# First expert layer of a four-layer model on one core: dense experts replaced by tiles of chosen token-expert pairs

## The reference, cut to what matters

```python
probs = softmax(xf @ gate_w.T)                    # 16 experts
_, idx = top_k(probs + gate_b, 6)                 # 6 of 16 per row
weights = take_along_axis(probs, idx)
for e in range(16):                               # hidden size 176
    h = silu(xf @ W1[e].T + B1[e]) * (xf @ W3[e].T + B3[e])
    y += cw[:, e:e+1] * (h @ W2[e].T + B2[e])     # cw is 0 where e was not chosen
y += shared(xf)                                   # hidden size 352, every row
```

## Time and profile before

| | us |
|---|---|
| median of 3 runs | 1162.48 |
| lowest, highest | 1162.35, 1163.56 |
| the profiled execution, its own time | 1165.65 |
| its span, first to last instruction | 1163.9 |
| PE busy (share of the span) | 990.9 (85%) |
| DVE busy | 672.4 (58%) |
| ACT busy | 354.6 (30%) |
| POOL busy | 353.8 (30%) |
| mean granted TensorE clock | 0.911 |

### The profile page before, as it was taken

How to read it: one execution, slowest core, us unless ns; L and a number is a source line. 1 busy time by engine, 2 the same in 40 slices (tenths; PEclk the granted TensorE clock), 3 DMA queues, 4 the chain that set the end, 5 groups by cost and what they waited for, 6 DMA issues and landing times. The chain is left out here.

```text
span 1163.9 us, 14272 instructions
## 1 busy us (share of the span) xinstructions
PE 990.9 (85%) x5133; PEld 795.6 (68%) x5133; DVE 672.4 (58%) x1105; ACT 354.6 (30%) x541; POOL 353.8 (30%) x244
## 2 busy tenths in 40 slices
PE   2999999868779999999788995967726869999996
PEld 2677787658568899998667894755615656566664
DVE  4466666545385556655634888968677853222221
ACT  2234443222522333333223442334313432222121
POOL 2577776400122222222100220153235310512222
PEclk9899999969889999999878996969956988999999
DMA  3111120001111111110081001000010019622220
GB/s 113 72 39 39 38 77 0 1 1 35 45 46 46 46 45 45 45 45 18 2 256 61 29 1 33 1 1 1 0 41 1 1 53 399 245 63 42 40 34 10
DMA packets 21473, 61.40 MB, mean 53 GB/s; under 512 B 4401, under 2 KB 12866, under 8 KB 19074
## 3 DMA queue, kind: packets, MB, share of 16 engines
q1 hardware_dynamic: 17346, 56.55, 14.3%
q0 software_dynamic: 4080, 4.22, 2.2%
HBM read 55.50 MB, written 9.21 MB: 56 GB/s over the span
## 5 line engine op out<-in xcount | busy, mean ns | idle before, releaser
L914 DVE SCALAR_TENSOR_TENSOR ffn_HF<-ffn_U,ffn_BIAS,ffn_HG 128x512 f32<-128x512 f32 x54 | 40.4, 750 | 82.5 <-ACT ffn_HG L797 82.4
L87 PE MATMUL ffn_DN<-ffn_WDS_hi,ffn_HS_hi 128*128 128x256 f32 x288 | 83.6, 290 | 3.9 <-DVE ffn_HS_lo L922 3.3
L797 ACT ACTIVATE ffn_HG<-ffn_G,ffn_UB 128x512 f32<-128x512 f32 x54 | 37.1, 690 | 160.5 <-PE ffn_U L89 160.1
L2160 PE MATMUL ffn_GU<-ffn_W,ffn_XTB 128*128 x184 | 85.0, 605 | 0.1
L88 PE MATMUL ffn_DN<-ffn_WDS_lo,ffn_HS_hi 128*128 128x256 f32 x288 | 83.3, 289 | 0.0
L89 PE MATMUL ffn_DN<-ffn_WDS_hi,ffn_HS_lo 128*128 128x256 f32 x288 | 83.2, 289 | 0.0
L767 POOL TENSOR_TENSOR ffn_WDS_lo<-ffn_WD,ffn_WDS_hi 128x1024 fp32r<-128x1024 f32 x9 | 22.1, 2461 | 200.2 <-ACT ffn_WDS_hi L787 200.2
L929 DVE SCALAR_TENSOR_TENSOR X<-ffn_DN,ffn_CG,X 128x256 f32<-128x256 f32 x144 | 67.3, 480 | 20.6 <-PE ffn_DN L89 12.5
L1980 POOL DMA_INDIRECT out_x<-ffn_YB,ffn_XB x23 | 35.9, 1560 | 113.7 <-DVE ffn_YB L2109 111.7
L464 DVE TENSOR_TENSOR attn_RP<-attn_QB,attn_COS 96x1024 f32<-96x1024 f32 x32 | 39.0, 1218 | 51.3 <-PE attn_QB L89 51.2
L2098 DVE COPY ffn_XTB<-ffn_XP 128x256 f32<-128x256 f32 x23 | 9.8, 425 | 88.0 <-PE ffn_XP L2169 88.0
(11 more groups left out here) (432 smaller groups left out, 2759.6 us busy)
## 6 DMA issues: line engine op xcount, KB each, us to landing
ffn_W<-in_f_w SPq DMA_DIRECT2D x9, 1536.0 KB, 27.9
attn_W<-in_L_pairs SPq DMA_DIRECT2D x8, 1088.0 KB, 5.0
ffn_WU<-in_f_up SPq DMA_DIRECT2D x9, 768.0 KB, 4.2
ffn_WD<-in_f_down SPq DMA_DIRECT2D x9, 512.0 KB, 3.5
expert_rows<-in_rows_empty SPq DMA_DIRECT2D x1, 2967.0 KB, 14.4
ffn_XB<-expert_rows SPq DMA_DIRECT2D x23, 129.0 KB, 2.1
ffn_STAGE<-in_f_w SPq DMA_DIRECT2D x1, 2048.0 KB, 8.2
ffn_STAGE<-in_L_pairs SPq DMA_DIRECT2D x2, 768.0 KB, 7.3
```

Source lines behind the costliest of these rows:

```text
L87: pe.matmul(out, a[0], b[0], start=first, stop=False)
L797: act.activation(HG[:, k % 2, :], G[:, k % 2, :], ACT.Silu, bias=bias).then_inc(silu_done, 1)
L914: dve.scalar_tensor_tensor(out=HF[:, k % 2, :], in0=U[:, k % 2, :], scalar=BIAS[:, bass.ds(e * (2 * NC) + 2 * m + 1, 1)], in1=HG[:, k % 2, ...
L2160: last = pe.matmul(GU[:, m, :], x, weights(e, k * 2 * HID3 + m * HID3, HID3), start=k == 0, stop=k == KD - 1)
```

## The change

`experts` is removed, and `routed_many` computes the same part by chosen pairs in plain float32. 8 items do the shared expert (hidden size 352, one tile of rows each). The 6144 pairs are sorted by expert into tiles of 128, at most 63 of them (`TILES0`). No rows are sorted in DRAM: XN is written out as it is, with the row's 16 weights behind it (`rows0`), and a list `IDX` of row numbers, 128 for each tile, is made on chip, by comparisons on DVE (`mark`, 8 of 128x2048 bf16) and 128 small matmuls on PE (`enlist`), while the shared items run. POOL gathers each tile's rows by that list with an indirect DMA, eight tiles ahead into twelve buffers, and scatters each result with addition, even tiles into `sum_a` (the residual with the shared part, written there first) and odd tiles into `sum_b` (zeros); a scatter waits for the one two before it. The last block of the layer ends when POOL has issued the last scatter. `latent_chain` then loads both sums, adds and measures them on DVE at the end of round 0, and takes the norm a round later. The order of a routed item on PE is up, turning the next rows, turning the hidden values of the item before, down for the item two before; on DVE bias, copy of the next rows, product; on ACT silu, copy, and the weighing of the item two before. Three DMAs from DRAM to DRAM (the table of layer 3, the zeros for `sum_b`, a zero row) go to SP's queue in the first attention block. The clearing after the int8 part goes, and one comes behind the first attention. The diff, cut to its core (the indents are cut too):

```diff
+E0, TOP0, HID0 = 16, 6, 176
+TILES0 = B * S * TOP0 // P + E0 - 1
+ROW0 = D + E0
+UP0 = KD * 2 * HID0
...
+    sp.dma_start(DR["rows3"][:, :], A["rows_empty"]).then_inc(scratch_set, 16)
+    sp.dma_start(DR["sum_b"][:, :], A["zeros"]).then_inc(scratch_set, 16)
+    sp.dma_start(DR["rows0"][B * S:B * S + 1, :], A["zero_row"]).then_inc(scratch_set, 16)
     with sp.Fori(1, NP) as p:
         sp.wait_ge(w_lo[2], p)
...
-    def experts(tag, gate, NE, NC, E, TOP, biased):
...
-    NORM_AFTER = 1
+    NORM_AFTER = 2
...
+    if g == 1:
+        for i, (dst, src) in enumerate(((X, "sum_a"), (XN, "sum_b"))):
+            sp.wait_ge(sums_done[i], 16 * ((TILES0 + 1 - i) // 2))
+            sp.dma_start(dst[:, :, :], DR[src].rearrange("(t p) d -> p t d", p=P)).then_inc(taken[i], 16)
...
+    if g == NORM_AFTER - 1:
+        act.wait_ge(measured, T)
+        nrm["deviation"](act)
     if g == NORM_AFTER:
         nrm["scalar"](act)
...
+    if g == 0:
+        for i in range(2):
+            dve.wait_ge(taken[i], 16)
+        for t in range(T):
+            dve.tensor_tensor(X[:, t, :], X[:, t, :], XN[:, t, :], ALU.add).then_inc(whole, 1)
+            dve.wait_ge(whole, t + 1)
+            measure(dve, stats, t).then_inc(measured, 1)
+    if g == NORM_AFTER - 1:
+        nrm["vector"](dve)
...
-    sp.dma_start(rows_dram[:, :], A["rows_empty"]).then_inc(xs_set, 16)
...
+    def routed_many(gate):
+        E, NT, NB, NY, HID, ROW = E0, TILES0, 12, 4, HID0, ROW0
+        ITEMS = T + NT
...
+    MARK_AT = {1: (0, 1), 2: (2, 3), 3: (4,), 4: (5,), 5: (6, 7)}
+    LIST_AT = {3: (0, 1), 4: (2, 3), 5: (4, 5), 6: (6, 7)}
...
+    sp.wait_ge(xn_ready, T)
+    sp.dma_start(DR["rows0"][0:B * S, 0:D].rearrange("(t p) d -> p t d", p=P), XN[:, :, :]).then_inc(rows_out, 16)
+    sp.dma_start(BIAS[:, :], A["f0_bias"]).then_inc(bias_in, 16)
+    for e in range(E):
+        sp.dma_start(W[:, e, :], A["f0_w"][e]).then_inc(w_in, 16)
+    sp.wait_ge(weights_ready, 1)
+    sp.dma_start(DR["rows0"][0:B * S, D:ROW].rearrange("(t p) d -> p t d", p=P), CW[:, :, :]).then_inc(weights_out, 16)
+    sp.wait_ge(shared_added, T)
+    sp.dma_start(DR["sum_a"].rearrange("(t p) d -> p t d", p=P), X[:, :, :]).then_inc(base_out, 16)
...
+    def gather(i):
+        if i >= NB:
+            pool.wait_ge(y_ready, i - NB + 1)
+            pool.wait_ge(x_turned, i - NB + 1)
+        pool.indirect_dma_start(XB[:, i % NB, :], None, DR["rows0"][:, :], bass.IndirectOffsetOnAxis(ap=IDX[:, i:i + 1], axis=0)).then_inc(rows_in[i % NB], 16)
+    def scatter(i):
+        pool.wait_ge(y_ready, i + 1)
+        if i >= 2:
+            pool.wait_ge(sums_done[i % 2], 16 * (i // 2))
+        pool.indirect_dma_start(DR["sum_b" if i % 2 else "sum_a"][:, :], bass.IndirectOffsetOnAxis(ap=IDX[:, i:i + 1], axis=0),
+                                YB[:, i % NY, :], None, bounds_check=B * S - 1, oob_is_err=False, compute_op=ALU.add).then_inc(sums_done[i % 2], 16)
+    pool.wait_ge(rows_out, 16)
+    pool.wait_ge(weights_out, 16)
+    pool.wait_ge(idx_ready, 1)
+    AHEAD = NB - 4
+    for i in range(AHEAD):
+        gather(i)
+    pool.wait_ge(base_out, 16)
+    for i in range(NT):
+        if i + AHEAD < NT:
+            gather(i + AHEAD)
+        scatter(i)
...
+    def weigh(n, e):
+        i = n - T
+        act.wait_ge(down_done, n + 1)
+        if i >= NY:
+            act.wait_ge(sums_done[i % 2], 16 * ((i - NY) // 2 + 1))
+        act.activation(YB[:, i % NY, :], DN[:, n % 2, 0:D], ACT.Copy, scale=XB[:, i % NB, bass.ds(D + e, 1)]).then_inc(y_ready, 1)
+    for n in range(ITEMS + 2):
+        if n < ITEMS:
+            silu(n)
+        if 1 <= n <= ITEMS:
+            h_copy(n - 1)
+        if n - 2 == T:
+            act.wait_ge(owners_out, 1)
+        if n - 2 >= T:
+            weigh(n - 2, act.value_load(EI[0:1, n - 2 - T:n - 1 - T], min_val=0, max_val=E - 1))
...
+    dve.tensor_tensor(OHA[:, t % NM, :, :], PLACESB[:, :, :],
+                      POSB[:, t, :].unsqueeze(1).broadcast_to((P, P, E)), ALU.is_equal).then_inc(places_marked, 1)
...
+    dve.tensor_tensor(GB[:, n % 2, :], GU[:, n % 2, 0:2 * HID], BIAS[:, bass.ds(e * (2 * HID), 2 * HID)], ALU.add).then_inc(biased, 1)
...
+    src = GU[:, 1, 0:2 * HID] if n < T else GB[:, n % 2, HID:2 * HID]
+    dve.tensor_tensor(h_rows(n)[:, 0:hidden(n)], src, HG[:, n % 2, 0:hidden(n)], ALU.mult).then_inc(h_full, 1)
...
+    dve.tensor_copy(XTB[:, n % 2, :], XP[:, 0:D]).then_inc(x_out, 1)
...
+    for n in range(ITEMS):
+        if n == T:
+            dve.wait_ge(bias_in, 16)
+        if n >= T:
+            add_bias(n, dve.value_load(EI[0:1, n - T:n - T + 1], min_val=0, max_val=E - 1))
+            if n + 1 < ITEMS:
+                x_copy(n + 1)
+        full(n)
+        if 2 <= n < T + 2:
+            finish(n - 2)
+        if n == 0:
+            place()
+        for t in MARK_AT.get(n, ()):
+            mark(t)
+        if n == 5:
+            owners()
+        if n == 6:
+            lists()
+        if n == T - 1:
+            x_copy(T)
...
+    for e in range(E):
+        last = pe.matmul(RL[:, e * 16:(e + 1) * 16], OHA[:, t % NM, :, e], OHB[:, t, e, :, :].rearrange("p h j -> p (h j)"),
+                         start=False, stop=t == T - 1 and e == E - 1, skip_group_check=True)
...
+        for m in range(2):
+            pe.matmul(GU[:, m, 0:2 * HID], ONES[0:1, :], BS[0:1, m, :], start=True, stop=False)
+            for k in range(KD):
+                at = k * 4 * HID + m * 2 * HID
+                last = pe.matmul(GU[:, m, 0:2 * HID], XTF[:, k, n * P:(n + 1) * P], WS[:, at:at + 2 * HID], start=False, stop=k == KD - 1)
+    else:
+        pe.wait_ge(x_out, n - T + 1)
+        for k in range(KD):
+            last = pe.matmul(GU[:, n % 2, 0:2 * HID], XTB[:, n % 2, k * P:(k + 1) * P], flat[:, bass.ds(e * WIDTH0 + k * 2 * HID, 2 * HID)], start=k == 0, stop=k == KD - 1)
...
+    pe.wait_ge(y_ready, n - T - 1)
...
+    for n in range(ITEMS + 2):
+        if n == T:
+            pe.wait_ge(w_in, 16 * E)
+            pe.wait_ge(owners_out, 1)
+        if n < ITEMS:
+            owner[n] = None if n < T else pe.value_load(EI[0:1, n - T:n - T + 1], min_val=0, max_val=E - 1)
+            up(n, owner[n])
+        if n == 0:
+            count()
+        for t in LIST_AT.get(n, ()):
+            enlist(t)
+        if n == T - 1:
+            index()
+        if n >= T and n + 1 < ITEMS:
+            turn_x(n + 1)
+        if 1 <= n <= ITEMS:
+            turn_h(n - 1)
+        if n >= 2:
+            down(n - 2, owner[n - 2])
+        if n == T - 1:
+            turn_x(T)
...
-    experts("f0", 4, 9, 3, 16, 6, True)
+    routed_many(4)
...
```

732 lines of the change are left out of this document (355 added, 377 removed).

## The result

The changed kernel takes 1176.13 us (median of 4 runs, 1175.47 to 1180.79) against 1162.99 for the kernel before (4 runs, 1162.35 to 1163.56): a ratio of 1.0113, with a 95% interval of 1.0084 to 1.0142. It is 1.1% slower where the prediction had it 1% faster. The profiled execution took 1175.47, with a span of 1173.7 against 1163.9, so 9.8 us more. The expert part (the feed-forward part of layer 0) starts at 285.2 before and 285.3 after.

A forecast was written before the change was run, and what follows sets the result against it. PE's matmuls bound the old stage; POOL at 3.12 us a tile would bind the new one. Stage terms gave 271.2 against 295.1 (-23.9), the chain block +11.5, total -12.4: 1150 us, range 1115 to 1190.

The forecast's parts named there:

- The forecast's own case: Routed loop of layer 0: POOL's pace of 3.12 us a tile binds; kernel 1150, own range 1138 to 1164, chance 0.5.
- norm, transposes, logits: Start of layer 0's expert part: takes 13.6 us at clock 0.55, as in the last layer.
- until the list is ready: Expert part, shared items on PE until the list of rows is ready in item 7: 55.0 us (50 to 62).
- from the list to the loop: Expert part, gather landing, two PE items, last finish and write of X to `sum_a`, before POOL's steady loop: 16.4 us.
- the loop: Routed tiles at POOL's pace: 63 scatters at 1.86 and 55 gathers at 1.26, 186.5 us.
- end of the loop to the next block: End of the expert part: the last 0.3 us of issue taken off the sum, nothing added.
- chain block, added: Chain block: adds and statistics after round 0 and the norm after round 1 cost net +11.5 us.
- all behind it: After the chain block: clearings balance and the last layer's table DMA goes, 0 us.
- The pace of a tile: Routed loop: POOL 3.12 us a tile (gather 1.26, scatter 1.86 with issue) against PE's 2.54.
- PE did not set the pace: Rival 1, routed loop: PE's 2.54 us a tile binds, stage 32 us earlier, kernel 1118; chance 0.12.
- The lead of 0.72 us behind a wait: Rival 2, routed loop: waits delay POOL's DMAs; scatters only 1180, gathers too 1207; chance 0.25 (0.15 and 0.10).
- DVE's products: Rival 3, routed loop: they hold up POOL 0.34 us a tile, 21 us in all, kernel 1171; chance 0.13.

The follow-up runs named there:

- the clearing on POOL: Changed kernel, with POOL clearing a 128x5120 float32 buffer after the last scatter of the expert block: 1185.20 us, one run.
- the first set: Runs of half gathers, missing bounds check, POOL's adds and the clearing on POOL, beside the kernel before (1164.57 to 1177.00 us over 19 runs).
- the experiment with one sum: Changed kernel, with each scatter waiting until the one before it has landed, not the one two before: 1263.91 us, one run.

## Why the prediction was wrong

The direction was wrong, by 22.2 us in the span (1151.5 forecast, 1173.7 measured), and no rival took over. The forecast's own case came about, and its sum was too short nearly everywhere. The steps, in the prediction's order:

| step | forecast | measured | |
|---|---|---|---|
| norm, transposes, logits | 13.6 | 13.6 | |
| until the list is ready | 55.0 (50 to 62) | 62.6 | +7.6 |
| from the list to the loop | 16.4 | 19.6 | +3.2 |
| the loop | 186.5 | 191.7 | +5.2 |
| end of the loop to the next block | -0.3 | 4.5 | +4.8 |
| chain block, added | 11.5 | 14.0 | +2.5 |
| all behind it | 0 | -1.2 | -1.2 |

**The largest step that failed is "Until the list of rows is ready"** (item 2 of the sum, forecast 55.0, measured 62.6). The up of the shared expert was priced at 3.69, twelve records at a slope without a fixed part; it takes 4.24, eight times 0.55 more, so 4.4. I allowed for one fall of the clock at 2.5 us; there were two, which cost 3.9 and 3.1, so 4.5 more. The small matmuls took 0.061 each and not 0.05, 1.4 more. PE waited only 1.8 us for DVE and not 5.1. Sum +7.0 of the 7.6. The small matmuls did not prove the main cause: doubling them showed their price, and that the clock can fall behind them. In the ten other executions of this stage one (in two of them), two (in four) or all three (in four) of the first three items ran at the lower clock, 3 to 4 us each, so how late the list comes is in part chance.

**The step that wasn't there is the end of the block.** The sum ended with POOL's last descriptor. It then takes 4.5 us, of which the last scatter's landing isn't the limit, as the clearing on POOL showed. The trace of before held the warning: a DRAIN of 3.25 us, at the very end of its last layer. I had read the end of POOL's queue there as the end of the work, because behind it there was nothing left to start. Ahead of a block that starts with 6 us of loading weights it counts in full. Why it takes 4.5 us stays open.

**The pace of a tile** was right in mechanism and nearly in size: 3.19 for 3.12. A gather cost 0.99 where 0.96 was taken, a scatter 1.60 where 1.56 was; over 63 tiles that is 4 us. One wait of 1.4 is the rest. The landing behind it was misread: the 2.72 of the earlier trace rows counts from the start of the instruction, not from the end of descriptor making, and was the shortest of 23, with a median of 3.7. That did no harm, as POOL comes back to a sum 6.4 us after the start of its last scatter into it. For PE 2.54 was wrong, 2.88 right, which did no harm only because POOL was slower still.

**From the list to the loop** the routed expert's first up ran at the lower clock, 2.7 us instead of 1.3, and the write of X to `sum_a` took 5.9 us from issue instead of the 4.4 of the earlier trace rows. Both lie ahead of the first scatter.

**The chain block.** Adds and statistics took 7.94 us for 8.2, the norm's products 1.38 as forecast. What was too low is the wait for the second sum (1.2, from the stated "0, at most 3"), and PE's restart at the lower clock behind the norm (622.01), 3.75 us for a group that took 1.99 there before. With 11.5 - 0.3 + 1.2 + 1.8 these give 14.2 of the measured 14.0. In the first set the block was 4 us longer still. The first attention block hid its three new DMAs, as counted: the expert part starts at 285.2 before and at 285.3 after.

**The rivals.** PE did not set the pace: halving the gathers gave 18 us. The lead of 0.72 us behind a wait didn't appear: before 58 of the 63 scatters POOL stood 0.30 us "for issue". DVE's products did not hold POOL up by their length, 0.34 us a tile and 21 us in all. The exclusive lock of the Trainium skill (SBUF — State Buffer, "SBUF: two separate sides") sets DVE's instructions with two SBUF inputs only against a GpSimd instruction that reads SBUF; it does not say that every product holds up the making of descriptors. The trace has a direct meeting: a product of this kind ran at 370.46, inside the gather that started at 370.22, and the gather took 0.95 us like the others ahead of the loop. Those in the loop took 0.99, and the scatters 1.60 between gathers and 1.56 behind the last gather, with DVE's products beside both. So as far as the rows show the 0.04 goes with the change between gather and scatter and not with DVE, whatever causes it. The prediction's 0.08 was not the only meeting either: in the trace of before a product of 0.69 us at 995.72 stood beside scatters of 0.96.

**The range** from 1115 to 1190 held 1176, but by luck: it was that wide for the rivals, and none of them came about. The forecast's own range, 1138 to 1164, missed by 12. The chances were wrong too: +7.6, +3.2, +5.2, +4.8 and +2.5 all have the same sign. The slack of each term had been listed (list 10, clock 6, loads 3 to 7) as if it could fall either way. Yet nearly every one of them was a wait or a restart that could only add, against a forecast gain of 12.4 us. The forecast's own case could therefore end slower than before, to which I had given no chance: nine tenths of it went to faster, the rest to no change, and the whole 0.38 for slower to the rivals.

## What to carry to other kernels

When the bound moves to another engine, follow it to the very end of its block: the time from its last instruction to the next block's first is a term of the sum, and the trace of before can show it where that engine ends a block. The terms of this sum were each priced at their undisturbed length, and every row of the table but the last came out longer or equal; ask of each term whether it can come out shorter, and set the chance of a loss by that. A duration that is read from one instruction can be the shortest of its kind: ask for the median. And a transfer of work from a busy engine to an idle one pays for its surroundings first: here the gathers' lead, the place of the adds and the loading of the next weights were together worth 10.7 us of the two stages in the traces and some 20 by the times, of a kernel that had lost 13, and the expert part and the chain block ended level with the kernel before. Last, an experiment's trace is best read against traces of its own set: the same chain block differed by 4 to 6 us between two sets.

## What the runs showed of the hardware that was not expected

- Where POOL had issued indirect DMAs in a block, ending it took 4.3 to 5.8 us in the expert part, also when POOL had computed for 4.4 us after the last of them. At the end of the last layer, before the change, it was 3.2 behind the last landing. Where POOL had only computed, it was 0.1, and behind a plain accumulating DMA the end came with the landing.
- An indirect DMA of 128 rows of 1 KB that accumulates mostly costs POOL 1.56 to 1.60 us, with or without a bounds check; one that gathers or scatters without accumulation 0.95 to 0.99, and 1.16 to 1.18 as the first of its kind.
- Accumulating scatters landed 2.7 to 4.0 us after the start of their instruction, 3.7 to 3.8 in the median. Two that waited for each other came 3.55 us apart where the landing was the shortest, and 4.68 in the experiment with one sum.
- An accumulating DMA of 1 MB from DRAM into SBUF costs POOL 1.6 us to issue and lands after 21.4 and 15.8 us.
- A float32 product over 49 rows is slower than one padded to 128: a down product of four records took 1.15 us with the 49 rows in its second half and 0.98 when padded.
- Comparing 128x2048 bf16 values on DVE took 1.22 us, not the 2.3 of the float32 slope; here the Trainium skill (VectorE: DVE Perf Modes, "Side-by-side"), which gives bf16 tensor_tensor twice the float32 rate, agrees with the trace.
- PE's granted clock was 1.00 over a first group of 64 matmuls of 16 columns and fell to its lower level (0.50) behind it, with no standstill; it also fell within the last of the four such groups, and not at the third (one run).
